# An attention and mixture-of-experts kernel on one core: expert results added to the output by indirect DMA, and 39 expert tiles in place of 46

## What is computed

```python
def xattn(query, kv):                      # query = layernorm(x)
    q = fmap(query @ Wq.T); gate = sigmoid(query @ Wg.T + bg)
    k, v = split(kv @ Wkv.T); k = fmap(k)  # fmap(a) = a + 1 if a > 0 else exp(a), 16 heads
    attn = (q @ (k.T @ v)) / (q @ k.sum + 1e-6)
    return attn * gate @ Wo.T
x = x + xattn(layernorm(x), ctx)           # "x2" in the kernel
h = layernorm(x)
w, sel = top_k(h @ Wr, 2); w = softmax(w)
out = x
for e in range(8):
    out += gate[..., e] * (h @ We[e] + be[e])   # gate: w spread over the two selected experts
```

## Time and profile before

| | us |
|---|---|
| median of 3 runs (600.34 to 603.24) | 601.4 |
| the profiled execution, its own time | 605.42 |
| its span, first to last instruction | 603.9 |

### The profile page before, as it was taken

The page is one execution under the profiler, slowest core; times in us unless marked ns, Lnnn a source line. Parts: engine busy times, 40 slices in busy tenths (PEclk is TensorE's granted clock), DMA queues, the critical chain, the costliest instruction groups (busy, mean ns, idle before and its releaser), DMA issues.

```text
span 603.9 us, 12871 instructions
## 1 busy us (share of the span) xinstructions
PE 546.0 (90%) x4192; PEld 443.9 (74%) x4193; DVE 323.3 (54%) x857; ACT 187.8 (31%) x340; POOL 170.9 (28%) x200
## 2 busy tenths in 40 slices
PE   6999999999999999999999999968799999958850
PEld 4778788878778887877887878856577888846640
DVE  4573367274357556337737537744466444437643
ACT  5455323434422333532343443321111111111100
POOL 4433453315540403632131430010130000156313
PEclk9999999999999999999999999998899999989885
DMA  8912533613541433363062258599566579589946
GB/s 280 363 39 106 174 140 112 238 71 125 192 170 40 162 118 106 144 199 112 0 245 71 79 198 316 198 384 415 189 216 187 163 236 296 160 266 314 380 172 188
DMA packets 44478, 114.18 MB, mean 189 GB/s; under 512 B 5008, under 2 KB 5008, under 8 KB 43536
## 3 DMA queue, kind: packets, MB, share of 16 engines
q1 hardware_dynamic: 24240, 57.43, 27.7%
q0 software_dynamic: 11264, 39.85, 18.9%
q10 hardware_dynamic: 8928, 16.26, 7.1%
HBM read 66.86 MB, written 46.66 MB: 188 GB/s over the span
## 4 chain that ended last, share of the span: by engine, by line
PE 82%; DMA 7%; issue 4%; DVE 3%; another core or an unknown queue 1%; ACT 1%; POOL 1%; SPq 0%; POOLq 0%; DVEq 0%; ACTq 0%
PE pj L1110 23%; PE pj L1112 22%; PE pj L1111 22%; PE tp L1102 5%; DMA khat<-xs 5%; PE tp L1177 3%; PE pj L1197 2%; PE kvb L1169 2%; PE pj L1119 1%; DMA wraw<-in_L_xattn_Wkv_dram 1%; DMA num<-y,gidx 1%; DVE R L809 1%; DVE R L818 1%; ACT R L648 0%
## 5 line engine op out<-in xcount | busy, mean ns | idle before, releaser
L1110 PE MATMUL pj<-R 128*128 128x512 f32 x448 | 184.4, 412 | 4.9 <-DVE R L818 4.3
L1112 PE MATMUL pj<-R 128*128 128x512 f32 x448 | 176.6, 394 | 0.0
L1111 PE MATMUL pj<-R 128*128 128x512 f32 x448 | 175.8, 392 | 0.0
L1110 PEld LDWEIGHTS pj<-R 128*128 128x128 f32 x448 | 84.9, 189 | 21.6 <-DVE R L818 4.5
L1112 PEld LDWEIGHTS pj<-R 128*128 128x128 f32 x448 | 84.6, 189 | 19.1
L1111 PEld LDWEIGHTS pj<-R 128*128 128x128 f32 x448 | 85.1, 190 | 15.2
L1110 PE MATMUL pj<-R,aux 128*128 x184 | 78.7, 428 | 9.5 <-DVE aux L822 6.6
L1111 PE MATMUL pj<-R,aux 128*128 x184 | 73.5, 399 | 0.0
L1112 PE MATMUL pj<-R,aux 128*128 x184 | 73.5, 399 | 0.0
L728 ACT CAST aux<-tp 128x512 fp32r<-128x512 f32 x46 | 26.9, 586 | 128.8 <-PE tp L1177 101.9
L818 DVE TENSOR_TENSOR R<-tp,R 128x512 fp32r<-128x512 f32 x64 | 43.8, 684 | 21.2 <-ACT R L648 21.2
(11 more groups left out here) (159 smaller groups left out, 677.0 us busy)
## 6 DMA issues: line engine op xcount, KB each, us to landing
we_halves<-aux POOLq DMA_DIRECT2D x14, 1024.0 KB, 5.1
R<-we_halves SPq DMA_DIRECT2D x7, 2048.0 KB, 11.1
khat<-xs SPq DMA_DIRECT2D x46, 256.0 KB
buf<-in_ctx_dram SPq DMA_DIRECT2D x15, 512.0 KB, 4.2
wraw<-in_L_ffn_We_dram POOLq DMA_DIRECT2D x14, 512.0 KB, 6.7
y<-kvbd ACTq DMA_DIRECT2D x23, 256.0 KB
y<-zeros ACTq DMA_DIRECT2D x23, 256.0 KB
wraw<-in_x_dram SPq DMA_DIRECT2D x4, 1024.0 KB, 8.1
```

Source lines behind the costliest of these rows:

```text
L1110: nc.tensor.matmul(bank[:, :], s_hi(k), m_hi(k), start=(k == 0), stop=False)
L1111: nc.tensor.matmul(bank[:, :], s_hi(k), m_lo(k), start=False, stop=False)
L1112: last = nc.tensor.matmul(bank[:, :], s_lo(k), m_hi(k), start=False, stop=(k == KT - 1))
```

## The change

The result of an expert tile is no longer stored and gathered. ScalarE multiplies it by the gate of each row, and GpSimd adds its 128 rows to the output in DRAM with an indirect DMA that accumulates. x2 is written to the output first. For this each row in `xs` gets 16 more numbers (width W = 528): its eight gates, its token number, and a mark for a padding row; `pay` reads them per tile. Padding rows must name a token too: one of the first 256 that the expert has not, found by `mark_pads`, 16 matmuls (step `C`) and `find_pads`.

The tiles are packed anew. Phase one is 13 tiles, all of them full and from the first three batches; phase two has the other 26, planned once all pairs are known. Unused tiles come first in phase two and read four `spare` blocks of zero rows.

Two tiles of one expert never name the same token. Tiles of different experts can, so an expert's first tile waits until every earlier addition has landed (`tile_alone`, 16 for such a tile and 0 for the others).

```diff
+    M0 = 13
+    M_ALL = PAIRS // P + E - 1
+    M1 = M_ALL - M0
+    assert ... and M_ALL == 39
+    XS, YS = 4, 4
-        START += [("L", "", 1), ("T", "z", 3)] + tiles(3) + [("K", "", 0)] + tiles(4) + [("L", "", 2)] + tiles(5)
-        START += [("K", "", 1)] + tiles(6) + [("L", "", 3)] + tiles(7) + [("K", "", 2)] + tiles(8) + [("K", "", 3)]
-        START += tiles(9) + tiles(10) + tiles(11) + tiles(12)
+        START += [("L", "", 1), ("T", "z", 3)] + tiles(3) + [("K", "", 0), ("L", "", 2)] + tiles(4)
+        START += [("K", "", 1), ("L", "", 3)] + tiles(5) + [("K", "", 2)] + tiles(6) + [("K", "", 3)]
+        for m in range(7, M_ALL):
+            START += tiles(m) + ([("C", "", 0)] if m == M0 - 2 else [])
 # SyncE
+            def load_tile(m):
+                row = sp.value_load(tile_row[0:1, m:m + 1], ...)
+                if m >= XS:
+                    sp.wait_ge(MOE["t_m"], mth(m - XS))
+                    sp.wait_ge(paid, m - XS + 1)
+                sp.dma_start(xs_raw[:, m % XS, :], xs_dram[bass.ds(row, P), :]).then_inc(xs_loaded[m % XS], 16)
...
+            for m in range(XS):
+                load_tile(m)
             sp.wait_ge(SEMS["g"], nth("g", B - 1, TT - 1))
             load_halves(4)
             load_halves(5)
-            load_tile(0, 2, 0)
+            load_tile(XS)
+            store_x2(B - 1)
             sp.wait_ge(SEMS["wo"], nth("wo", B - 1, TT - 1))
-            load_tile(0, 3, 1)
             load_halves(6)
-            load_tile(0, 4, 0)
+            load_tile(XS + 1)
             load_halves(7)
...
 # GpSimd
+            pool.wait_ge(zeroed, 1)
+            for s in range(YS):
+                pool.dma_start(xs_dram[bass.ds(E * ROWS + s * P, P), :], zeros[:, :]).then_inc(added[s], 16)
...
+            def add_rows(m):
+                slot = m % YS
+                if m == 0:
+                    pool.wait_ge(x2_stored, 16 * B)
+                if m == M0:
+                    pool.wait_ge(x2_stored, 16 * B + 16)
+                pool.wait_ge(y_scaled, m + 1)
+                if m >= 1:
+                    alone = pool.value_load(tile_alone[0:1, m:m + 1], min_val=0, max_val=16)
+                    for d in range(1, min(m, YS - 1) + 1):
+                        pool.wait_ge(added[(m - d) % YS], alone + 16 * ((m - d) // YS + 1))
+                nc.gpsimd.indirect_dma_start(out=out_rows[:, :], out_offset=...out_idx[:, m % (2 * YS)...],
+                                             in_=y_sb[slot], in_offset=None, compute_op=ALU.add).then_inc(added[slot], 16)
+            for step, kind, i in START:
+                if step == "M" and i >= 2:
+                    add_rows(i - 2)
+                elif step == "K":
+                    scatter(last, i)
...
 # ScalarE: bias_in(t) loads be[4 + t] behind x2's tile t; bias_in(3) stands behind ("T", "z", 0)
+            def scale_y(m):
+                act.wait_ge(MOE["y_copied"], mth(m))
+                nc.scalar.activation(y_sb[m % YS], y_sb[m % YS], ACT.Identity, scale=w_sel[...]).then_inc(y_scaled, 1)
 # VectorE
+            def pay(m):
+                e = dve.value_load(tile_expert[0:1, m:m + 1], ...)
+                nc.vector.tensor_scalar(w_sel[:, n:n + 1], row[:, bass.ds(e + GATES, 1)], 1.0, None, ALU.mult)
+                nc.vector.scalar_tensor_tensor(out_idx[:, n:n + 1], pad_token[...], row[:, PADDED:PADDED + 1], row[:, TOKEN:TOKEN + 1],
+                                               ALU.mult, ALU.add).then_inc(paid, 1)
+            def copy_y(m):
                 dve.wait_ge(MOE["m_done"], mth(m))
+                if m >= YS:
+                    dve.wait_ge(added[m % YS], 16 * (m // YS + 1))
+                nc.vector.tensor_tensor(y_sb[m % YS], pj[m % 2][:, :], be_all[...], ALU.add).then_inc(MOE["y_copied"], 1)
             for step, kind, i in START:
                 if step == "T" and kind == "m":
                     low_m(i, i % 2)
+                    pay(i)
                 elif step == "M":
-                    copy_y(i, i % 2, i // 2)
+                    copy_y(i)
+                    if 7 <= i < 10:
+                        next(planning, None)      # plan_rest, in three parts of 14, 14 and 7 small steps
+                    if 9 <= i < 12:
+                        next(marking, None)       # mark_pads: 6 small steps, then twice 8 compares of 128 x 128 bf16
 # TensorE
+                elif step == "C":
+                    pe.wait_ge(pads_marked, 2)
+                    for t in range(2):
+                        for e in range(E):
+                            last = nc.tensor.matmul(pj[2][:, t * E + e:t * E + e + 1], marks[:, t, e, :], token_b[:, t:t + 1], ...)
+                    last.then_inc(pads_found, 1)
```

More of the change, by code:

```diff
@@ L111, in xattn_moe_kernel @@
         w_raw += [gate[:, :, :], qhat[:, :, :], w_raw[0]]
[L112 to L118, removed]
+        normed = sb("normed", [P, 2, W])
+        rows = [normed[:, 0, :], normed[:, 1, :], num[:, 0, :], num[:, 1, :]]
+        xn = [r[:, 0:D] for r in rows]
         ident = sb("ident", [P, P])
@@ L126, in xattn_moe_kernel @@
         iota8 = sb("iota8", [P, E])
-        iota_t = sb("iota_t", [P, max(TILES)])
-        steps = sb("steps", [P, max(GROUP_TILES)])
+        iota_t = sb("iota_t", [P, M1])
+        free_rows = sb("free_rows", [P, -(-M1 // YS), YS])
+        free_row = free_rows[:, :, :].rearrange("p a s -> p (a s)")[:, 0:M1]
+        spare = sb("spare", [P, YS, E + 2])
+        steps = sb("steps", [P, STEPS])
+        token = sb("token", [P, 2])
+        token_b = sb("token_b", [P, 2], BF16)
+        place_p = sb("place_p", [P, P], BF16)
         below = sb("below", [P, E, E])
@@ L149, in xattn_moe_kernel @@
         rank_t = sb("rank_t", [P, 2])
[L150 to L154, removed]
+        run = sb("run", [P, E])
         xidx = sb("xidx", [P, TT, 2], U32)
-        gidx = sb("gidx", [P, 4, 2], U32)
+        w_sel = sb("w_sel", [P, 2 * YS])
+        out_idx = sb("out_idx", [P, 2 * YS], U32)
+        used = sb("used", [P, 1 + E])
+        shift_e = sb("shift_e", [P, E])
         nt = sb("nt", [P, 1 + E])
@@ L357, in _ @@
                 ctx_pair(b + 1, 3)
[L359 to L368, removed]
@@ L454, in passed @@
                 pool.sem_inc(pool_passed, 1)
-            nc.gpsimd.memset(zeros[:, :], 0.0).then_inc(zeroed, 1)
+            link(nc.gpsimd.memset(zeros[:, :], 0.0))
+            nc.gpsimd.memset(zeros[:, PADDED:PADDED + 1], 1.0).then_inc(zeroed, 1)
             link(nc.gpsimd.memset(ident[:, :], 0.0))
@@ L598, in _ @@
-            halves_in(7)
-            for t in range(TT):
-                scatter(1, last, t)
-            def gather(g, c, slot):
-                pool.wait_ge(gidx_done, c + 1)
-                pool.wait_ge(combined, c + 1)
-                passed()
-                for j in range(2):
-                    nc.gpsimd.indirect_dma_start(out=yg[slot][j], out_offset=None, in_=y_dram[g][:, :],
-                                                 in_offset=bass.IndirectOffsetOnAxis(ap=gidx[:, slot, j:j + 1], axis=0)).then_inc(gathered[slot], 16)
@@ L628, in _ @@
+            for step, kind, i in START:
+                if step == "M":
+                    if i == M0 + 2:
+                        pool.wait_ge(planned, 2)
+                    if i >= 2:
+                        add_rows(i - 2)
+                elif step == "K":
+                    scatter(last, i)
+            add_rows(M_ALL - 2)
+            add_rows(M_ALL - 1)
+            for s in range(YS):
+                pool.wait_ge(added[s], 16 * ((M_ALL - 1 - s) // YS + 2))
         @block.scalar
@@ L932, in queries @@
                             low_m(0, 0)
+                            pay(0)
                         else:
```

491 lines of the change are left out of this document (224 added, 267 removed).

## The result

The changed kernel takes 583.9 us, median of 4 runs (583.34 to 587.78); on the same chip the kernel before takes 601.4. The ratio is 0.972, 95% interval 0.967 to 0.977: faster, by 17.4 us where 45.4 were forecast, and 1.9 us above the upper end of the range. The profiled execution spans 582.4 us against a forecast of 558.3, so 24.1 us are to be found. Ratios and times leave out the slow executions: two of six in the last run of the changed kernel (`e18`) and one of six (745.6 us) in `e9`. The page of the changed kernel, against the earlier trace rows: span, busy time, the granted clock in 40 slices, and the new group of additions (busy us, mean ns, idle time before them).

What follows compares the result with a forecast made beforehand. TensorE, busy 90% of 603.9 us, was taken as the bound: last matmul 525.0 before waits, plus 10 + 8 + 6 + 8.3 + 1 gives a 558.3 span; plus 1.5 minus 4.0, 556 us. Range 538 to 582.

Steps and rivals of the forecast that it cites:

- the seven tiles: Expert tiles on TensorE: 39 in place of 46, each 3.18 us, saving 22.3 us, all on the path.
- the start: Start of the expert tiles: taken as unchanged at about 394.7 us, with tiles 0 to 3 loaded ahead of the weights.
- L: Time of one accumulating DMA from start to landed data: taken as 5.5 us, between 3.6 and 7.76.
- The bias row: First expert tiles: last bias row makes `copy_y(0)` some 5 us late, hidden by tile 1; 0, up to 3 us.
- The weights' stall: Before tile 5 or 6: rows queued behind experts' weights on SyncE stall TensorE 6.5 to 12 us; 10 taken.
- Planning and step `C`: Tiles 7 to 10 and after: VectorE's planning and padding, then 16 small matmuls waiting; 6 to 10 us, 8 taken.
- The additions: Expert tiles: 14 waits on GpSimd, each putting it back 2.3 us, mostly recovered; 6 us of stall taken.
- Rival B: Additions in the expert tiles are long under load, L = 7.5, costing 26 in place of 6: 578 us; chance 0.17.
- DMA engines: Steady expert tiles: additions raise the DMA share from 0.51 to 0.76 or 1.0; no stall counted.
- Attention: Attention: VectorE's operations balance; four DMAs of zeros in the first 30 us cost 1 us, 0 to 3.
- The end: After the last matmul: copy, scaling, GpSimd's start, one landing and 1 us of backlog; 8.3 us in place of 22.3.
- A: Rival: additions in the expert tiles are cheap, L = 3.6, no wait binds: 544 us; chance 0.20.

Runs made afterwards that it cites:

- e18: The changed kernel as it is, run again on a chip of the faster kind: 576.7 us, ratio 0.9755 to the kernel before.
- e9: Changed kernel plus the three mends, with GpSimd waiting only for additions that share a token, listed as constants for these inputs: 569.2 us, ratio 0.942.
- e3: Changed kernel with the final wait for the additions on SyncE and not on GpSimd: 579.1 us, ratio 0.976 to the kernel before.
- the three mends: Changed kernel with late biases awaited at tile 4, rows of tiles 10 to 12 before the padding, last wait on SyncE: 578.1 us (0.958); again 577.2 (0.9746).

## Why the prediction was wrong

Right were the sign, the seven tiles, the start and the size of L. The forecast for TensorE's last matmul was 550.0 and it ended at 566.2; the end was 8.3 and took 16.2. Point by point, on the changed kernel's own trace (the four stretches by the starts of tiles 0, 4, 10, 13 and 38):

- **The bias row, costed at 0, up to 3.** It cost 6.4 us up to tile 4. VectorE waited 8.0 us, not 5, and for all bias rows at once. I named tile 1 as cover, but VectorE stands in `copy_y(0)`, and behind it on its queue is the cutting of the next tile's rows (L792), for which TensorE waits 3.75 us and then runs at 1.2 GHz for 12 matmuls.
- **The weights' stall, 10, before tile 5 or 6.** In the changed kernel it doesn't show, as the tiles are late already. It showed at 3.4 + 1.6 us once the bias rows were mended. What stands there instead is the **step I had not read**: SyncE's wait for the counts ahead of tile 10's rows. From tile 4 to 10 were lost 13.8 us, against 10.
- **Planning and step `C`, 8.** 7.0 from tile 10 to 13, which comes near by luck. Tile 10 itself took 2.6 of it, at the lower clock behind its stall; planning and `C` took 4.3, with gaps of 1.2 and, ahead of the 16 matmuls, 2.2, and 0.55 for these.
- **The additions, 6.** 11.7 from tile 13 to 38 and 2.8 in the last tile. The mechanism was the one described; the failed term is its price at a wait. I took the landing time L = 5.5 for the distance of two starts. A single landing was indeed 5.2 to 5.6 us, but from one start to the next it is 6.66: additions caught up in a row land later, up to 6.9, and behind the landing GpSimd needs 0.9 us more for its waits and the plan's next value. Rival B's sum with 6.66 is 14 x 3.48 - 24 x 1.3 - (5.6 - 1.2) = 13. The 6 was no result of that sum, which is below 0 with 5.5, but set by hand for the bunches. GpSimd's own step of 1.9 was right in sum only: 1.55 and 0.30 stand where I added 0.95 and 0.88. The second fault was to treat stalls in phase one as if they added to this.
- **DMA engines, 0.** Right for TensorE, which is not held back beside 0.95; they only lengthen landings after a burst, above.
- **Attention, 1.** The tiles start 0.4 us earlier than before.
- **The end, 8.3.** 5.4 us from the last matmul to the last addition's start, where 2.8 were summed, since three additions stand behind the wait at tile 36. The transfer took 4.9. Then 5.9 us in which no engine and no DMA works, costed at nothing. What they consist of was not found out. With the last wait on SyncE they were about 3, and the tail, from the last addition's start, 8.1 to 8.4 instead of 11. That difference is too small to show in the times of `e3`.

Together, each against its forecast: 6.4 + 3.8 - 1.0 + 8.5 - 1.4 = 16.3 on TensorE (16.2 without the rounding) and 7.9 at the end, 24.1. That is a reading of where TensorE stood still. By the experiments it is not the price of each stall: without the bias stall or the stall of tile 10 the time is the same within the intervals, since other chains run beside both: late rows, the counts and the plan up to tile 13, and the additions behind it. Of the rivals, B had the right mechanism with too large a figure (7.5; 578). A falls with 4.6 us for an addition by itself.

Open stays what the three mends are worth, why they brought 8 to 9 us on one chip and nothing on another, and what alone would shorten the 30 us from tile 7 to 13.

## What to carry to other kernels

When transfers are put in order by waits, price a wait by the distance between two starts, landing plus all that the issuing engine does before it starts the next, and compare the whole chain of them with the bounding engine's pace, over the stretch and not for each wait. Read every in-order queue through to its end: a wait that guards a small transfer also holds the large one behind it. And a stall seen on the busiest engine is worth its length only if no second chain runs beside it, and it may also hand the time on to the next late transfer; remove it and look at the end before counting it.

## Not expected of the hardware

An indirect DMA that adds costs GpSimd 1.55 us to issue, 0.59 more than one that stores; it lands after 4.6 to 5.0 us with nothing else running against 2.7 for one that stores, and holds the DMA engines 1.96 us against 0.69. And the span went on for about 6 us behind the last transfer when GpSimd waited for it, for about 3 when SyncE did.
